# Second-step splits moved into the loop's first turns, clips moved to ScalarE, third map chunk moved ahead of the second attention step

## The reference

```
x = x + L0(_gn(x), ...)      # _gn: per image and channel, subtract the mean, divide by the deviation
x = x + L1(_gn(x), ...)
L0: fa, fb = bn(conv3x3(x))                       # 16 channels each
    att_a = bn(conv1x1([fa, gh, gw]))             # position planes gh, gw, pr
    map_a = sigmoid(conv3x3([att_a, gh, gw, pr]))
    out   = [fa * map_a * scale1, fb * map_b * scale2]
L1: offs = conv3x3(x) -> off_y, off_x (9 taps each);  mask = 2 * sigmoid(conv3x3(x))
    sampled = bilinear_gather(x, y + tap + off_y, x + tap + off_x) * mask
    out = einsum("nckhw,ock->nohw", sampled, weight) + bias; batch norm over (n, h, w); relu
```

## Time and profile before

| | us |
|---|---|
| median of 3 runs | 334.38 (334.09 to 335.42) |
| profiled execution | 333.83 |
| its span, first to last instruction | 332.1 |
| mean granted TensorE clock | 0.967 |

### The profile page before, as it was taken

How to read it: one execution, slowest core, us unless ns; L and a number is a source line. 1 busy time by engine, 2 the same in 40 slices (tenths; PEclk the granted TensorE clock), 3 DMA queues, 4 the chain that set the end, 5 groups by cost and what they waited for, 6 DMA issues and landing times. The chain is left out here.

```text
span 332.1 us, 16311 instructions
## 1 busy us (share of the span) xinstructions
PE 261.9 (79%) x7285; PEld 179.3 (54%) x7286; DVE 271.7 (82%) x513; ACT 238.7 (72%) x352; POOL 210.9 (64%) x162
## 2 busy tenths in 40 slices
PE   0379996888985887887899999898989998898340
PEld 0357431432533665656666777676667666667330
DVE  4743378833679999999999999999999998999776
ACT  1321355462879499988799999999989998997116
POOL 9200033500416778898789989998998998898400
PEclk9999997999999799999999999999999999999695
DMA  7891000000130220220000012000000210000006
GB/s 260 159 219 31 2 3 0 13 13 2 40 73 15 42 59 5 111 62 5 4 5 4 4 39 111 4 5 5 2 6 4 109 39 6 4 4 5 4 0 253
DMA packets 11956, 14.35 MB, mean 43 GB/s; under 512 B 4269, under 2 KB 7918, under 8 KB 11848
## 3 DMA queue, kind: packets, MB, share of 16 engines
q1 hardware_dynamic: 10137, 11.49, 11.8%
q10 hardware_dynamic: 1667, 1.19, 1.8%
q0 software_dynamic: 80, 0.61, 0.9%
HBM read 4.73 MB, written 2.98 MB: 23 GB/s over the span
## 5 line engine op out<-in xcount | busy, mean ns | idle before, releaser
L1467 DVE TENSOR_TENSOR prod<-ps,hy 128x480 f32<-128x480 f32 (+1 forms) x256 | 138.1, 601 | 7.9 <-PE ps L869 1.7
L869 PE MATMUL ps<-zreg,hx 64*64 64x96 f32 x4608 | 124.6, 249 | 19.6 <-DVE prod L1467 11.0
L609 POOL TENSOR_TENSOR prod<-prod 128x832 f32<-128x832 f32 x64 | 128.6, 2010 | 17.3 <-DVE prod L1467 15.1
L869 PEld LDWEIGHTS ps<-zreg,hx 64*64 64x64 f32 x4608 | 110.0, 134 | 38.0 <-ACT hx L1130 29.4
L1020 ACT ACTIVATE hx<-ps 128x576 f32<-128x576 f32 x129 | 77.0, 650 | 17.9 <-PE ps L749 15.8
L1130 ACT ACTIVATE hx<-hx,rbias 128x1152 f32<-128x1152 f32 x63 | 79.9, 1268 | 0.4
L613 POOL TENSOR_TENSOR prod<-prod 128x320 f32<-128x320 f32 x64 | 50.6, 791 | 5.0
L1475 DVE TENSOR_REDUCE areg<-prod 128x64 f32<-128x576 f32 x64 | 48.5, 758 | 2.6 <-POOL prod L613 0.6
L749 PE MATMUL ps<-wz,xpad 32*64 32x144 f32 (+1 forms) x1024 | 35.3, 322 | 3.1 <-issue 1.5
L585 POOL TENSOR_TENSOR x_sb<-prod,x_sb 128x512 f32<-128x512 f32 x8 | 10.1, 1268 | 43.0 <-DVE prod L1305 43.0
L1125 ACT ACTIVATE zreg<-ps 128x576 f32<-128x576 f32 x56 | 37.0, 661 | 0.0
(11 more groups left out here) (158 smaller groups left out, 259.9 us busy)
## 6 DMA issues: line engine op xcount, KB each, us to landing
zreg<-zreg SPq DMA_DIRECT2D x12, 288.0 KB, 2.4
out<-x_sb SPq DMA_DIRECT2D x7, 256.0 KB, 2.1
x_sb<-in_x SPq DMA_DIRECT2D x3, 512.0 KB, 4.7
preg<-scratch SPq DMA_DIRECT2D x14, 54.0 KB
zreg<-in_pos POOLq DMA_DIRECT2D x1, 528.0 KB, 5.0
x_sb<-in_x SPq DMA_DIRECT2D x2, 256.0 KB, 6.8
scratch<-parts SPq DMA_DIRECT2D x12, 36.0 KB
scratch<-prod SPq DMA_DIRECT2D x11, 36.0 KB
```

Of the source, the lines that this page charges most:

```text
L609: pool.tensor_tensor(slots[:, :, 0:2 * moved], slots[:, :, 0:2 * moved], slots[:, :, 2 * KEPT:6 * KK], ALU.add).then_inc(half_folded, 1)
L869: return pe.matmul(g_ps(g, h)[u * W:(u + 1) * W, k - TAPS[h][0], :, :], hx[s, (t + u) % 4, k, :], z_sb[s, b, at:at + 3, k * C:(k + 1) * C] ...
L1467: mul = vector.tensor_tensor(pv[:, n0:n1], gv, wv[:, n0:n1], ALU.mult)
```

## The change

The third map chunk (`c == 2`) gets PSUM bank 0, and `prod` a third slot. TensorE and ScalarE do chunks 0 to 2 ahead of the second attention step; DVE multiplies chunks 0 to 2 and takes statistics 0 ahead of its six copies, then product 3, statistics 1 and 2, and from chunk 4 on product and statistics in turn.

In the loop, DVE keeps only `split_rest` of images 0 and 1 ahead of it. The others go into turns 0 to 4, the vertical weights into turns 3 to 8, the reaches into turns 9 and 10. The casts of the mid parts of images 2 and 3 on POOL go behind the folds of turns 1 and 3. ScalarE makes the vertical inputs in turns 1 to 4 and does the three clips, as `Relu(-2 x)`, in turns 6, 8 and 10. POOL clears the far tables behind the fold of turn 11.

```diff
--- before.py
+++ after.py
@@ -368,6 +368,11 @@
         CLOSES = tuple(n for n in range(ZRING, ZROWS, ZRING))
 
 
+        def map_bank(c):
+
+            bank = 0 if c == 2 else 2 + c % 2
+            return ps[:, bank * BANK:(bank + 1) * BANK]
+
         def att_piece(s, j, dy):
 
             r = (SPREAD * s + j) * CH_ROWS + 2 - dy
@@ -582,16 +587,20 @@
             for c in range(NCH):
                 pool.wait_ge(sig_used, c + 1 + CREDIT)
                 x_c = x_sb[:, c * BANK:(c + 1) * BANK]
-                pool.tensor_tensor(x_c, prod[:, c % 2, 0:BANK], x_c, ALU.add).then_inc(x1_ready, 1)
+                pool.tensor_tensor(x_c, prod[:, c % 3, 0:BANK], x_c, ALU.add).then_inc(x1_ready, 1)
+
+            def split_mid(s, b):
+
+                pool.wait_ge(rest_ready, B * s + b + 1)
+                pool.tensor_copy(parts[s][:, 1, b, :], rest[s][b]).then_inc(mid_ready, 1)
 
             for s in range(STEPS):
                 for b in range(B + 1):
                     if b < B and s > 0:
                         pool.wait_ge(cv_saved, B * s + b + 1)
                         pool.tensor_copy(part(s, 0, b), rows_of(offc[s][:, b, :])).then_inc(high_ready, 1)
-                    if b > 0:
-                        pool.wait_ge(rest_ready, B * s + b)
-                        pool.tensor_copy(parts[s][:, 1, b - 1, :], rest[s][b - 1]).then_inc(mid_ready, 1)
+                    if b > 0 and (s == 0 or b <= 2):
+                        split_mid(s, b - 1)
 
             far_row = pool.alloc_register("far_row")
 
@@ -612,7 +621,9 @@
                 pool.wait_ge(half_folded, i + 1)
                 pool.tensor_tensor(slots[:, :, 0:2 * moved], slots[:, :, 0:2 * moved],
                                    slots[:, :, 2 * SUMMED:2 * KEPT], ALU.add).then_inc(folded, 1)
-                if i == 9:
+                if i in (1, 3):
+                    split_mid(1, 2 + i // 2)
+                if i == 11:
                     wait_stored(pool, 2)
                     pool.memset(far_tables, 0.0).then_inc(far_zeroed, 1)
 
@@ -662,8 +673,9 @@
                 low, high = att_pieces(c)
                 pe.wait_ge(att_saved, 3 * low + CREDIT)
                 pe.wait_ge(att_shifted, 3 * high)
-                pe.wait_ge(sig_used, c + (CREDIT - 1))
-                pe.matmul(ps[:, (2 + c % 2) * BANK:(3 + c % 2) * BANK], mapw,
+                if c > 2:
+                    pe.wait_ge(sig_used, c + (CREDIT - 1))
+                pe.matmul(map_bank(c), mapw,
                           attrep[:, c * CH_ROWS + 1:(c + 1) * CH_ROWS + 1, 0:W],
                           start=True, stop=True).then_inc(map_ready, 1)
 
@@ -688,10 +700,10 @@
             conv_taps(1, range(4, KK)).then_inc(conv_ready, 1)
             pe.wait_ge(mapw_ready, 1)
             pe.wait_ge(pos_loaded, 16 * 2)
-            map_chunk(0)
-            map_chunk(1)
+            for c in range(3):
+                map_chunk(c)
             att_step(1)
-            for c in range(2, NCH):
+            for c in range(3, NCH):
                 map_chunk(c)
             pe.wait_ge(ones_ready, 1)
             pe.wait_ge(map_loaded, 16 * (3 + 3 * len(MAP_PIECES)))
@@ -985,10 +997,9 @@
                                    ps[:, c * BANK:(c + 1) * BANK].rearrange("p (r x) -> p r x", x=W),
                                    ACT.Identity, bias=col(BB), scale=col(BS)).then_inc(f_ready, 1)
 
-            def sigmoid_map(c, u):
+            def sigmoid_map(c):
                 act.wait_ge(map_ready, c + 1)
-                act.activation(ps[:, (2 + u) * BANK:(3 + u) * BANK], ps[:, (2 + u) * BANK:(3 + u) * BANK],
-                               ACT.Sigmoid).then_inc(sig_ready, 1)
+                act.activation(map_bank(c), map_bank(c), ACT.Sigmoid).then_inc(sig_ready, 1)
 
             def shift_att(s):
 
@@ -1002,11 +1013,11 @@
             save_branches(0)
             shift_att(0)
             save_branches(1)
-            sigmoid_map(0, 0)
-            sigmoid_map(1, 1)
+            for c in range(3):
+                sigmoid_map(c)
             shift_att(1)
-            for c in range(2, NCH):
-                sigmoid_map(c, c % 2)
+            for c in range(3, NCH):
+                sigmoid_map(c)
             act.activation(warm[:, 3:4], warm[:, 0:1], ACT.Sqrt).then_inc(warmed, 1)
             root(3)
             act.wait_ge(shift_ready, 2)
@@ -1131,8 +1142,12 @@
                                    ACT.Relu, bias=rbias[:, 0:1], scale=-1.0).then_inc(hx_ready, 2)
                 else:
                     weights(NT, 2)
-                if 3 <= i < 7:
-                    vertical(1, i - 3)
+                if 1 <= i < 5:
+                    vertical(1, i - 1)
+                elif i in (6, 8, 10):
+                    r = i // 2 - 3
+                    act.wait_ge(hy_half, 6 + 2 * r + 2)
+                    act.activation(hy_step(r, 1), hy_step(r, 1), ACT.Relu, scale=-2.0).then_inc(hy_ready, 1)
 
                 m = i - MAKERS + 1
                 if m == 0:
@@ -1298,16 +1313,13 @@
 
             def add_branches(c):
 
-                u = c % 2
                 vector.wait_ge(sig_ready, c + 1 + CREDIT)
-                if c >= 2:
-                    vector.wait_ge(x1_ready, c - 1)
-                vector.scalar_tensor_tensor(prod[:, u, 0:BANK].rearrange("p (r x) -> p r x", x=W),
-                                            ps[:, (2 + u) * BANK:(3 + u) * BANK].rearrange("p (r x) -> p r x", x=W), p_(V_SCALE),
+                if c >= 3:
+                    vector.wait_ge(x1_ready, c - 2)
+                vector.scalar_tensor_tensor(prod[:, c % 3, 0:BANK].rearrange("p (r x) -> p r x", x=W),
+                                            map_bank(c).rearrange("p (r x) -> p r x", x=W), p_(V_SCALE),
                                             f_sb[:, c * CH_ROWS:(c + 1) * CH_ROWS, 1:1 + W],
                                             ALU.mult, ALU.mult).then_inc(sig_used, 1)
-                if c > 0:
-                    statistics(c - 1)
 
             def statistics(c):
 
@@ -1318,11 +1330,16 @@
             save_branches(0)
             save_att(0)
             save_branches(1)
-            add_branches(0)
-            add_branches(1)
+            for c in range(3):
+                add_branches(c)
+            statistics(0)
             save_att(1)
-            for c in range(2, NCH):
+            add_branches(3)
+            statistics(1)
+            statistics(2)
+            for c in range(4, NCH):
                 add_branches(c)
+                statistics(c - 1)
             vector.wait_ge(codes_made, 1)
             chain(vector.tensor_copy(tile_col[:, :], ps[:, 6 * BANK + P128:6 * BANK + P128 + 1]))
             vector.tensor_scalar(later[:, :], ps[:, 6 * BANK:6 * BANK + P128], tile_col[:, :], None, ALU.is_le)\
@@ -1413,10 +1430,6 @@
                 save_offsets(b)
             for b in range(2):
                 split_rest(1, b)
-            for b in range(2):
-                split_low(1, b)
-                vector.wait_ge(parts_ready, B + b + 1)
-                split_rest(1, b + 2)
             vector.wait_ge(hy_ready, 3)
 
             at_reach = ps[:, REACH_AT:REACH_AT + P128]
@@ -1479,16 +1492,15 @@
             for i in range(NT // 2):
                 weigh(i, 0)
                 weigh(i, 1)
-                if i < 2:
-                    split_low(1, i + 2)
-                elif i < 4:
-                    reaches(i - 2)
-                elif 4 <= i < 13:
-                    r, part_of = (i - 4) // 3, (i - 4) % 3
-                    if part_of < 2:
-                        vertical_weights(1, 2 * r + part_of)
-                    else:
-                        vertical_rest(1, r)
+                if i in (0, 2, 3, 4):
+                    split_low(1, (0, 2, 3, 4).index(i))
+                if i in (1, 2):
+                    vector.wait_ge(parts_ready, B + i)
+                    split_rest(1, i + 1)
+                if 3 <= i < 9:
+                    vertical_weights(1, i - 3)
+                elif i in (9, 10):
+                    reaches(i - 9)
                 elif i == MAKERS + 5:
                     first = first_far(vector)
                     vector.wait_ge(first_tent, 1)
```

## The result

The changed kernel takes 337.91 us (median of 4 runs, 336.72 to 338.55) beside 334.24 (334.07 to 335.42) for the kernel before: ratio 1.0108, 95% interval 1.0073 to 1.0143. It is slower. Run again later beside others (12 runs) it took 337.39 against 334.17, ratio 1.008 (1.0048 to 1.0113). The profiled execution took 338.55, its span is 336.8 against 332.1.

The account below looks back on a forecast made before the run. Bound by DVE's turns locked with POOL's folds, 3.02 us each late in the loop. Loop +2.75 and map phase +0.15 make 333.83 into 336.7; with 0.55 to the median, 337.3 us, range 335.8 to 338.7 (332.8 to 338.8 with rival 1).

Parts of the forecast that it names:

- The start: Loop start: W(0), turn 0's first product, at 103.3 against 107.26; W(1) at 106.5, W(2) at 110.1.
- The port: Turns 3, 4: POOL's fold goes between two DVE port operations (splits, weights, clips), 5.8 us a turn; no-hand-over rival 4.1, 14%.
- Turn 2: Loop turn 2: POOL's cast or DVE's low split first, too close to call; price 1.8 or 0.15 us.
- the first case: Turn 2 with POOL's cast first: W(3) at 116.3, W(15) at 162.1 against 158.50, +3.6 us.
- The clearing: POOL's far-table clearing behind fold 11 delays fold 12 in a bare turn: +1.35 us; rival, covered by slack, 6%.
- From turn 15 on nothing differs: Loop from turn 15: no further gain or loss, the loop's cost taken as W(15)'s shift, +2.75 us.
- my range's 0.6 for clock and clearing: Margin of 0.6 us beyond turn 2's two cases, giving 335.8 to 338.7 us.
- Clips: Three clips moved to ScalarE, turns 6, 8, 10: hidden, cost nothing; saving 3 x 0.39 us in DVE's bare turns.
- The map phase: Ahead of the loop: chunk 4 starts at 54.1 instead of 53.94, +0.15 us; rival with 2.4 GHz clock -1.1, 8%.
- The sum: Whole kernel: +2.75 in the loop and +0.15 in the map phase, +2.9 us.
- the middle of turn 2's two cases: W(15) taken between +3.6 (cast first) and +1.9 (low split first): +2.75 us.

Follow-up runs that it names:

- The order of the weights alone: Kernel before, with each row's two vertical weights in one turn (5, 8, 11) instead of one each in two turns: 338.63 us, ratio 1.0143.
- the part alone: Kernel before with only the change's map part (third chunk ahead of the second attention step): 332.94 us, ratio 0.996; again 333.32 us, ratio 0.9966.
- the spread kernel: Change's loop part re-ordered: at most one split, weight or clip a DVE turn, clearing in four pieces, map phase as before; 330.48 us, ratio 0.9879 to kernel before.
- the spread kernel with the map part: The spread kernel with the map part of the change added: 330.98 us, ratio 0.9897 against the kernel before.
- four-piece: Changed kernel, but POOL clears the far tables in four pieces behind the folds of turns 6 to 9: 336.19 us, ratio 1.0042 to kernel before.

## Why the prediction was right

- *The start.* Forecast W(0) 3.96 sooner. From the second normalization it is 37.92 instead of 41.74: 3.8. TensorE kept 2.4 GHz from 102 to 116.4, as forecast for the first turns; then, while it waited for turn 3's products, it fell to 1.2 GHz until 126.7. W(1) and W(2) came 3.04 and 6.78 behind W(0), forecast 3.2 and 6.8.
- *The port.* Forecast turns 3 and 4 at 5.8, measured 5.69; the second operation 2.3 us. The order of the weights alone is worth 1.4% in the kernel before, clock included, and taking the second port operation out of turns 3 and 4 took 3.0 us out of these two turns and, with the clock behind it, the loss out of the median. That POOL is served between two such operations of DVE, when its own was issued before the second of them, is shown; why the chip does so was not examined.
- *Turn 2.* I had called it open between 1.8 and 0.15. The cast came first (111.64 against 111.84), and in all five profiles with this order the turn took 6.14 to 6.16. The median lay 0.6 above my forecast at first and 0.1 on the second measurement, though the first case should have put it 0.85 above.
- *The clearing.* Forecast 1.35, measured 1.1 to 1.2, but its slack was mis-sized: behind two turns with reaches it costs nothing. What followed it, 1.7 us of half clock in turns 15 to 17 of three of the four profiles with the pause, was not in the sum, which has "From turn 15 on nothing differs"; my range's 0.6 for clock and clearing was too little for it.
- *Clips.* Hidden, as forecast; worth 0.6% (0.3 to 0.9), where I had booked 1.2 us, which is within the interval.
- *The map phase.* Forecast +0.15. Counted from chunk 0, chunk 4 started at 9.92 in the changed kernel's profile against 9.99, but the clock fell at 51.6 and not at 54.0, and the phase took 0.39 more. Yet the part alone came out 0.3 to 0.4% faster in medians, twice. The profiles don't show how. From chunk 0 to the second normalization the old order took 21.57, 21.30 and 21.39 with a clock fall and 20.35 three times without one; the new order had a fall in all seven profiles, and took 20.88 to 22.05. By that it should be slower. This stays open, and so does whether it adds anything to the spread kernel.
- *The sum.* +2.9 forecast, +3.7 and +3.2 measured. The step that is off by size is the loop's: 0.4 less than its first case at W(15), and 1.7 more from the clock behind it, perhaps offset in part by a map phase that is better in medians than I had it; that offset is not shown.
- *Luck.* The mechanism of turns 2 to 4 was right, but that the median came within 0.6 and 0.1 is partly luck. The sum took the middle of turn 2's two cases, which no execution can show, it left out the clock behind turn 13, and it had the map phase with the wrong sign for the medians. For the profiled execution I had 336.7; it took 338.55.

## What to carry to other kernels

Before putting two VectorE operations in a row beside a busy GpSimd, look whether both are of the kind that met it in these rows (here splits and weights, with two SBUF inputs) and how long GpSimd's next operation is: if it is issued before the second one, the second one pays that length, and the profile books it as VectorE's busy time. With one such operation a turn, with a reduce or a product from PSUM between, turns 0 to 11 of the spread kernel took 3.06 to 3.80. The changed kernel and the spread kernel with the map part differ in this order, in the turns of the hidden clips and in the clearing, which cost nothing in the spread kernel: ratio 1.008 to 1.011 against 0.990. And work that stalls the chain for over a microsecond can have a second price, TensorE's clock some microseconds later: 1.7 us in three of four profiles here.

## What the runs showed of the hardware

- A VectorE operation's recorded duration contains its wait for GpSimd: 0.56 us of work recorded as 2.31, 0.69 as 2.33. The sum of busy times grew by 1.9 us while three operations left.
- A memset by GpSimd didn't lengthen the VectorE weights beside it: 0.57 beside the 1.49 us one of the kernel before (weight issued at 143.81), 0.57 to 0.58 beside the 0.45 us pieces of the four-piece and spread kernels. What it held up was GpSimd's own next fold (154.55 in the changed kernel).
- TensorE's granted clock differs between executions of one kernel. The changed kernel's first profile is at 0.50 from 116.4 to 126.7, its second from 116.4 to 119.8 and from 123.2 to 133.5. The spread kernel's profile never fell before the loop's end (span 326.9, clock 0.977); other executions of it took up to 2.8 us more, at 0.963. The mean clock was 0.941 to 0.959 with the changed kernel and 0.947 to 0.976 with the kernel before (0.967 in its profile).
